# Cross-attention with MLP: scores from two float32r parts in half of the array's rows, each score matmul beside a row-maximum matmul

## The chip, the core and the metric

One core of a Trainium2 chip runs the kernel in one launch. Its engines run their own instruction streams and meet at semaphores: TensorE (PE in the profile, with its weight loads as PEld), VectorE (DVE), ScalarE (ACT), GpSimd (POOL), and SyncE (SP), which here issues all the DMAs. The metric is the device time of a run in microseconds, less is better, as the median of several runs.

## The reference

```python
qn = _layer_norm(Q, ln_q_g, ln_q_b)
q = (qn @ Wq + bq).reshape(B, Lq, H, DH).transpose(0, 2, 1, 3)
k = (KV @ Wk + bk).reshape(B, Lkv, H, DH).transpose(0, 2, 1, 3)
v = (KV @ Wv + bv).reshape(B, Lkv, H, DH).transpose(0, 2, 1, 3)
scores = jnp.einsum('bhqd,bhkd->bhqk', q, k) / jnp.sqrt(jnp.float32(DH))
attn = jax.nn.softmax(scores, axis=-1)
ctx = jnp.einsum('bhqk,bhkd->bhqd', attn, v)
ctx = ctx.transpose(0, 2, 1, 3).reshape(B, Lq, D)
x = Q + (ctx @ Wo + bo)
h = _layer_norm(x, ln_ff_g, ln_ff_b)
ff = jax.nn.silu(h @ W1 + b1) @ W2 + b2
return x + ff
```

All arrays are float32: 16 batches, 512 queries, 1601 keys, width 256, 16 heads of 16 numbers, an MLP of width 1024.

## The kernel before

The main loop has 16 batches of four quarters. A quarter is four heads: for each of 13 tiles of 128 keys (the last has 65) it makes scores with keys on the partitions and 512 queries along the row, two heads at a time. Such a half tile is a **unit**, so a quarter has 26 units and a batch 104. ScalarE takes the exponential of a unit (L717, 128x1024); after the second unit of a tile, TensorE multiplies the previous tile's probabilities by V (L1029, "pv"): four heads side by side in four groups of 32 array columns, float32.

The exponential needs the maximum of each query's scores subtracted. So TensorE makes the scores a second time, with queries on the partitions (L995, `make_rows`, in chunks of 512 keys, 52 steps for a quarter, every thirteenth of them four short products with the 65 last keys), into the two buffers of `rows_ps`, and VectorE reduces each step to a maximum (L830, `read_rows`). These maxima belong to the next quarter, or the one behind it; four steps fall to each key tile. In unit 19 VectorE negates and splits the finished maxima, in unit 22 TensorE turns them (kind "turn", L944), ScalarE copies them out, and SP places them by DMA as extra rows of `q_stack` (`place_shift`, L424), where the next quarter's first scores wait for them (`shift_landed`).

A float32 product of scores is made in bfloat16: q and k are each split into three bfloat16 parts (ScalarE writes `whole` and the first part, GpSimd subtracts for the others, L513 to L516), and the six products of parts that matter are stacked along the contraction: 6 x 16 = 96 rows, plus three for the shift. SP gathers the parts head by head into `k_stack` and `q_stack` (`place`, L389) and then copies the repeated ones (`repeat`, L401).

Every other product (projections k, q, v, output, both MLP layers, and transposes) is a float32 **side product** through one PSUM tile `side`, with an evacuation by ScalarE or VectorE. Tables give each a range of units. `plan` writes out TensorE's order: per key tile the scores, side products and pv, and between them the four maximum steps, spread evenly by the table `COST`. TensorE runs this order strictly: `make_rows` waits until VectorE has read the step before the last, `make_scores` until the exponential before the last is done.

A prologue prepares the first batch and its first maxima; an epilogue finishes the last batch's output and MLP.

Of the kernel before, what the change touches and what calls it, by code (L numbers as in the profile page):

```python
# [27 lines left out]
F32 = mybir.dt.float32  # L28
BF16 = mybir.dt.bfloat16
# [28 lines left out]
PLACED = 2 * 4 * PARTS  # L58
REPEATED = 2 * (len(K_ROWS) - PARTS)
# [64 lines left out]
def products(kind, arg):  # L124
# [4 lines left out]
    first, second = {"turn": (QT, 1), "x": (QT, 1), "k": (1, KC), "q": (1, KC), "wo": (2, 4), "h": (KC, 2), "w1": (2, KC), "w2": (2, FM)}[kind]  # L129
# [39 lines left out]
COST = {"scores": 512, "pv": 2048, "v": 512, "ctx": 256, "x": 256, "h": 256, "turn": 128, "k": 2048, "q": 2048,  # L169
        "wo": 1024, "w1": 1024, "w2": 1024}  # L170


def plan(steps):


    units, slot = [], 0
    for t in range(KT):
        work = []
        for u in (2 * t, 2 * t + 1):
            work += [(u, "scores", j) for j in range(2)]  # L180
            work += [(u, "side", product) for product in products_at(steps, u)]
            work += [(u, "pv", None)] * (u % 2)
        costs = [COST[what[1] if kind == "side" else kind] for _, kind, what in work]
        done, placed, tile = 0, 0, {2 * t: [], 2 * t + 1: []}
        for (u, kind, what), cost in zip(work, costs):
            tile[u].append((kind, what))
            done += cost
# [43 lines left out]
def xattn_kernel(nc, x, ctx, wq, bq, wk, bk, wv, bv, wo, bo, w1, b1, w2, b2, gq, cq, gf, cf, out):  # L231
    with ExitStack() as stack:
# [27 lines left out]
        rest = sb("rest", [P, CHUNK])  # L260
        k_parts = sb("k_parts", [P, PARTS, LK], BF16)
        q_parts = sb("q_parts", [P, PARTS, LQ], BF16)
# [100 lines left out]
        def _(sp):  # L363
# [70 lines left out]
            def prologue():  # L434
# [19 lines left out]
                for c in (2, 3):  # L454

                    sp.wait_ge(side_ready, index(PREPARE[1], "ctx", (c - 2, KC - 1)) + 1)
                    load_ctx(0, c)
# [659 lines left out]
```

## Time and profile before

| | us |
|---|---|
| runs: median of 3 (lowest to highest) | 3768.38 (3765.79 to 3769.14) |
| the profiled execution's own time | 3763.43 |
| its span, first to last instruction | 3761.6 |
| prologue, loop, epilogue (about) | 145, 3538, 79 |
| PE, DVE, ACT busy | 3559.0, 2483.2, 2242.9 |

Busy time counts an engine's instructions; waits on semaphores are not in it. A matmul's recorded duration contains the latency through the array, so the rate is read from starts: two matmuls in a row that start 0.22 us apart cost 0.22 us each, whatever their own duration says. Each float32 matmul stands in the trace as two records.

### The profile page before, as it was taken

The numbers are of one execution on the slowest core, as the hardware profiler recorded it, in microseconds if no ns is written. First come the engines' busy times: TensorE is split into PE (matmuls) and PEld (weight loads), VectorE is DVE, ScalarE is ACT, GpSimd is POOL, SyncE is SP. The second block draws the span as 40 slices with busy tenths as digits, with TensorE's granted clock in tenths as the row PEclk, the third lists the DMA queues.
The fourth block names the chain that finished last, engine by engine and source line by source line (L and its number), as shares of the span: only waits on it lengthen the run. The fifth ranks groups of instructions, "written<-read, shape, count | busy, mean of one in ns | idle before, by whom it ended". The sixth has DMA issues, their size and how long they took to land.

```text
span 3761.6 us, 52959 instructions
## 1 busy us (share of the span) xinstructions
PE 3559.0 (95%) x19880; PEld 1605.0 (43%) x19880; DVE 2483.2 (66%) x4568; ACT 2242.9 (60%) x2979; POOL 901.5 (24%) x1323
## 2 busy tenths in 40 slices
PE   3899999999999999999999999999999999999996
PEld 2233444444434444444444434444444444444434
DVE  2777767666676766667666676766667676676751
ACT  1366666656666565666656666566656656666562
POOL 2122313212231222313122231212313112231101
PEclk8899999999999999999999999999999999999999
DMA  3222212222122321212222122322212232121200
GB/s 84 45 50 40 46 32 61 41 47 45 32 51 39 65 41 32 47 33 58 41 58 38 30 50 37 64 41 36 49 32 54 42 64 39 27 48 34 41 7 12
DMA packets 121409, 162.99 MB, mean 43 GB/s; under 512 B 36912, under 2 KB 102464, under 8 KB 118080
## 3 DMA queue, kind: packets, MB, share of 16 engines
q1 hardware_dynamic: 121152, 159.60, 21.7%
q8 instruction: 157, 2.57, 0.3%
q14 instruction: 100, 0.82, 0.1%
HBM read 46.43 MB, written 8.39 MB: 15 GB/s over the span
## 4 chain that ended last, share of the span: by engine, by line
PE 81%; DVE 11%; ACT 4%; issue 2%; SPq 1%; POOL 1%; DMA 0%; ACTq 0%; POOLq 0%; DVEq 0%
PE o_ps L1029 20%; PE rows_ps L995 19%; PE scores L1010 14%; DVE chunk_max L830 8%; PE side L972 6%; PE side L969 6%; PE side L958 5%; PE side L950 4%; PE side L962 3%; ACT probs L717 2%; PE side L954 2%; DVE stats L748 1%; DVE resid L775 1%; PE side L941 1%; ACT ctxT L633 1%
## 5 line engine op out<-in xcount | busy, mean ns | idle before, releaser
L830 DVE TENSOR_REDUCE chunk_max<-rows_ps 128x1 f32<-128x512 f32 (+1 forms) x3328 | 2124.4, 666 | 1132.9 <-PE rows_ps L995 1124.4
L717 ACT ACTIVATE probs<-scores 128x1024 f32<-128x1024 f32 (+1 forms) x1664 | 1676.0, 1023 | 1174.5 <-PE scores L1010 1167.1
L995 PE MATMUL rows_ps<-k_stack,q_stack 96*128 96x512 bf16 (+1 forms) x4096 | 1220.1, 339 | 94.1 <-DVE chunk_max L830 50.6
L1010 PE MATMUL scores<-q_stack,k_stack 99*128 99x512 bf16 (+1 forms) x3328 | 1033.6, 379 | 3.3 <-ACT probs L717 2.7
L1029 PE MATMUL o_ps<-probs,v_sb 128*32 128x512 f32 x6656 | 886.5, 605 | 0.4 <-ACT probs L717 0.4
L995 PEld LDWEIGHTS rows_ps<-k_stack,q_stack 96*128 96x128 bf16 x4096 | 334.3, 97 | 1164.2 <-DVE chunk_max L830 930.7
L1010 PEld LDWEIGHTS scores<-q_stack,k_stack 99*128 99x128 bf16 (+1 forms) x3328 | 325.0, 100 | 300.4 <-issue 38.2
L513 POOL TENSOR_TENSOR rest<-whole,k_parts 128x512 f32<-128x512 f32 (+1 forms) x128 | 120.6, 942 | 1002.4 <-ACT k_parts L663 997.2
L565 POOL TENSOR_TENSOR attT<-o_sb,denom 128x512 f32<-128x512 f32 x64 | 81.2, 1268 | 945.3 <-DVE denom L817 945.3
L969 PE MATMUL side<-hT,w_sb 128*128 128x256 f32 x1024 | 272.6, 380 | 11.8 <-ACT tanh_sb L675 9.9
L972 PE MATMUL side<-w_sb,ffT 128*128 128x256 f32 x1024 | 259.2, 381 | 5.6 <-DVE ffT L793 5.0
L1029 PEld LDWEIGHTS o_ps<-probs,v_sb 128*32 128x32 f32 x6656 | 131.0, 108 | 296.8 <-issue 222.2
L958 PE MATMUL side<-wv_sb,ctxT 128*128 128x128 f32 (+1 forms) x1664 | 242.3, 278 | 4.6 <-ACT v_sb L649 2.0
L958 PEld LDWEIGHTS side<-wv_sb,ctxT 128*128 128x128 f32 (+1 forms) x1664 | 226.0, 187 | 46.7 <-ACT v_sb L649 11.4
L950 PE MATMUL side<-ctxT,wk_sb 128*128 128x512 f32 (+1 forms) x512 | 222.7, 519 | 9.2 <-ACT k_parts L663 9.2
L969 PEld LDWEIGHTS side<-hT,w_sb 128*128 128x128 f32 x1024 | 192.9, 190 | 63.2 <-ACT tanh_sb L675 17.0
L972 PEld LDWEIGHTS side<-w_sb,ffT 128*128 128x128 f32 x1024 | 191.5, 189 | 56.5 <-issue 7.7
L673 ACT ACTIVATE ffT<-side,half_b 128x256 f32<-128x256 f32 x256 | 121.5, 475 | 111.5 <-PE side L969 108.8
L528 POOL TENSOR_TENSOR newton<-rstd 128x2 f32<-128x2 f32 (+1 forms) x144 | 28.1, 195 | 591.6 <-DVE half_var L763 584.0
L962 PE MATMUL side<-wo_pad,attT 128*128 128x256 f32 x512 | 139.7, 389 | 5.0 <-POOL attT L565 3.9
L675 ACT ACTIVATE tanh_sb<-side,half_b 128x256 f32<-128x256 f32 x256 | 121.7, 475 | 0.0
L514 POOL TENSOR_TENSOR k_parts<-whole,k_parts 128x512 bf16<-128x512 f32 (+1 forms) x128 | 121.1, 946 | 0.1
(68 smaller groups left out, 1971.3 us busy)
## 6 DMA issues: line engine op xcount, KB each, us to landing
k_stack<-k_parts SPq DMA_DIRECT2D x768, 50.0 KB, 2.2
k_stack<-k_stack SPq DMA_DIRECT2D x192, 200.1 KB, 5.6
ctx_nat<-in_ctx SPq DMA_DIRECT2D x48, 512.0 KB, 4.0
q_stack<-q_parts SPq DMA_DIRECT2D x768, 16.0 KB, 1.8
q_stack<-q_stack SPq DMA_DIRECT2D x192, 64.0 KB, 3.4
x_nat<-in_x SPq DMA_DIRECT2D x16, 512.0 KB, 6.1
resid<-in_x SPq DMA_DIRECT2D x32, 256.0 KB, 2.8
out<-resid SPq DMA_DIRECT2D x32, 256.0 KB, 2.5
```

The source lines that it names most:

```text
L673: nc.scalar.activation(ffT[:, m, :], side[:, cols], ACT.Identity, bias=half_b1[:, m:m + 1], scale=0.5)
L675: last = nc.scalar.activation(tanh_sb[:, cols], side[:, cols], ACT.Tanh, bias=half_b1[:, m:m + 1], scale=0.5)
L717: nc.scalar.activation(probs[0:rows, (q + t) % 2, 2 * LQ * pair:2 * LQ * (pair + 1)], scores[0:rows, 2 * LQ * pair:2 * LQ * (pair + 1)], A ...
L830: nc.vector.tensor_reduce(dst, src, AX.X, ALU.max).then_inc(rows_read, 1)
L950: ins = nc.tensor.matmul(side[:, 0:width(arg)], wk_sb[:, j, P * s:P * (s + 1)], ctxT[:, j, CHUNK * arg:CHUNK * arg + width(arg)], start=(j ...
L958: ins = nc.tensor.matmul(side[0:rows, P * t:P * (t + 1)], ctxT[:, j, P * i:P * i + rows], wv_sb[:, j, P * s:P * (s + 1)], start=(j == 0), ...
L962: ins = nc.tensor.matmul(side[:, D * i:D * (i + 1)], attT[:, j, q0:q0 + P], wo_pad[:, j, :], start=(j == 0), stop=(j == 3))
L969: ins = nc.tensor.matmul(side[:, QH * i:QH * (i + 1)], w1_sb[:, j, P * m:P * (m + 1)], hT[:, j, :], start=(j == 0), stop=(j == KC - 1))
L972: ins = nc.tensor.matmul(side[:, D * i:D * (i + 1)], ffT[:, j, P * i:P * (i + 1)], w2_sb[:, j, :], start=(j == 0), stop=(j == FM - 1))
L995: last = nc.tensor.matmul(rows_ps[:, m % 2, d0:d0 + w], q_stack[s][0:STACK, h, P * t:P * (t + 1)], k_stack[s][0:STACK, h, k0:k0 + w], star ...
L1010: ins = nc.tensor.matmul(scores[0:keys_in(t), LQ * j:LQ * (j + 1)], k_stack[s][:, h, P * t:P * t + keys_in(t)], q_stack[s][:, h, :], start ...
L1029: last = nc.tensor.matmul(o_ps[32 * j:32 * j + 32, :], v_sb[q // 2][0:rows, t, col:col + 32], probs[0:rows, (q + t) % 2, LQ * j:LQ * (j + 1)],
```

## The change

q and k are split into two float32r parts (4 bytes each) in place of three bfloat16 ones; three products of parts are stacked, 48 rows plus two for the shift. A head then needs only half of the array's 128 rows: even heads stand in partitions 0 to 49 of the stacks, odd heads in 64 to 113. The maximum steps alternate between the halves. In each unit TensorE issues scores of the odd head, a maximum step of an even head, scores of the even head, a maximum step of an odd head; then pv in every second unit; then all of the unit's side products. The copies of repeated parts (`repeat`) are gone, since `place` now places all three; `place_shift` issues four DMAs in place of three; GpSimd has one subtraction in place of three per chunk; VectorE's negation has three instructions in place of seven; a turn is one float32 transpose in place of four bfloat16 matmuls. The short maximum products have 66 keys in place of 65.

```diff
-PARTS = 3
-K_ROWS = (0, 0, 0, 1, 1, 2)
-Q_ROWS = (0, 1, 2, 0, 1, 0)
+PARTS = 2
+K_ROWS = (0, 0, 1)
+Q_ROWS = (0, 1, 0)
 STACK = 16 * len(K_ROWS)
 ROWS = STACK + PARTS
+HALF = 64
+PAIRS = HH // 2
...
-TAIL = width(NCH - 1)
-M_STEPS = [step for r in range(M_ROWS) for step in [(r, c) for c in range(NCH - 1)] + [(r, None)] * (r % 4 == 3)]
+TAIL = width(NCH - 1) + 1
+M_STEPS = [step for p in range(2) for step in
+           [(e, p, t, c) for t in range(QT) for c in range(NCH - 1) for e in range(2)] + [(e, p, None, None) for e in range(2)]]
...
+PARTNER = (1, 0, 1, 0)
...
-    units, slot = [], 0
+    units = []
     for t in range(KT):
-        work = []
-        for u in (2 * t, 2 * t + 1):
-            work += [(u, "scores", j) for j in range(2)]
-            work += [(u, "side", product) for product in products_at(steps, u)]
-            work += [(u, "pv", None)] * (u % 2)
...
-            while placed < PER_TILE and done * PER_TILE >= (placed + MAX_PHASE) * sum(costs):
-                tile[u].append(("max", slot))
-                placed, slot = placed + 1, slot + 1
-        units += [tile[2 * t], tile[2 * t + 1]]
+        for n, u in enumerate((2 * t, 2 * t + 1)):
+            unit = []
+            for k in (2 * n, 2 * n + 1):
+                unit += [("scores", PARTNER[k]), ("max", PER_TILE * t + k)]
+            units.append(unit + [("pv", None)] * n + [("side", product) for product in products_at(steps, u)])
     return units
...
-        k_parts = sb("k_parts", [P, PARTS, LK], BF16)
-        q_parts = sb("q_parts", [P, PARTS, LQ], BF16)
-        k_stack = [sb(f"k_stack{s}", [ROWS, HH, LK], BF16) for s in range(2)]
-        q_stack = [sb(f"q_stack{s}", [ROWS, HH, LQ], BF16) for s in range(2)]
+        k_parts = sb("k_parts", [P, PARTS, LK], F32R)
+        q_parts = sb("q_parts", [P, PARTS, LQ], F32R)
+        k_stack = [sb(f"k_stack{s}", [P, PAIRS, LK], F32R) for s in range(2)]
+        q_stack = [sb(f"q_stack{s}", [P, PAIRS, LQ], F32R) for s in range(2)]
...
-                for part in range(PARTS):
-                    slot = rows.index(part)
+                for slot, part in enumerate(rows):
                     for h in range(4 * (g % 2), 4 * (g % 2) + 4):
-                        sp.dma_start(dst[16 * slot:16 * slot + 16, h, :], src[16 * h:16 * h + 16, part, :])\
...
+                        first = HALF * (h % 2) + 16 * slot
+                        sp.dma_start(dst[first:first + 16, h // 2, :].bitcast(F32),
+                                     src[16 * h:16 * h + 16, part, :].bitcast(F32)).then_inc(placed[g], 16)
...
                 place(k_stack[s], k_parts, K_ROWS, 2 * s + 1)
-                repeat(b, 2 * s)
                 place(q_stack[s], q_parts, Q_ROWS, 2 * s + 1)
-                repeat(b, 2 * s + 1)
...
-                for i in range(PARTS):
-                    sp.dma_start(q_stack[q // 2][STACK + i:STACK + i + 1, 4 * g:4 * g + 4, :],
-                                 shift_parts[4 * i:4 * i + 4, :])\
-                        .then_inc(shift_landed, 16)
+                for e in range(2):
+                    for i in range(PARTS):
...
-                wait(pool, split, b * 10 + n)
-                seq.inc(nc.gpsimd.tensor_tensor(rest[:, 0:w], src, first, ALU.subtract))
-                seq.inc(nc.gpsimd.tensor_tensor(second, src, first, ALU.subtract))
-                pool.wait_ge(pool_seq, seq.value)
-                nc.gpsimd.tensor_tensor(parts[:, 2, off:off + w], rest[:, 0:w], second, ALU.subtract).then_inc(split, 1)
+                nc.gpsimd.tensor_tensor(parts[:, 1, off:off + w], whole[:, n % 2, 0:w],
+                                        parts[:, 0, off:off + w].bitcast(F32), ALU.subtract).then_inc(split, 1)
...
-                    ins = nc.tensor.matmul(side[0:4 * PARTS, P * i:P * (i + 1)],
-                                           neg_parts[:, i, :, :].rearrange("p a h -> p (a h)"), ident_bf[:, :],
-                                           start=True, stop=True)
+                    ins = nc.tensor.transpose(side[0:PARTS * M_ROWS, 0:P],
+                                              neg_parts[:, :, :].bitcast(F32).rearrange("p a r -> p (a r)"), ident[:, :])
...
-                for row in [r] if c is not None else range(r - 3, r + 1):
-                    t, h = row // 4, 4 * (q % 2) + row % 4
-                    k0, w, d0 = (CHUNK * c, CHUNK, 0) if c is not None else (CHUNK * (NCH - 1), TAIL, TAIL * (row - r + 3))
-                    last = nc.tensor.matmul(rows_ps[:, m % 2, d0:d0 + w], q_stack[s][0:STACK, h, P * t:P * (t + 1)],
-                                            k_stack[s][0:STACK, h, k0:k0 + w], start=True, stop=True)
+                for tile in [t] if c is not None else range(QT):
+                    k0, w, d0 = (CHUNK * c, CHUNK, 0) if c is not None else (LK - TAIL, TAIL, TAIL * tile)
+                    last = nc.tensor.matmul(rows_ps[:, m % 2, d0:d0 + w], q_stack[s][rows, pair, P * tile:P * (tile + 1)],
+                                            k_stack[s][rows, pair, k0:k0 + w], start=True, stop=True)
...
-                j = 2 * (u % 2) + n
-                h = 4 * (q % 2) + j
+                j, pair, rows = 2 * (u % 2) + n, 2 * (q % 2) + u % 2, slice(HALF * n, HALF * n + ROWS)
                 ins = nc.tensor.matmul(scores[0:keys_in(t), LQ * j:LQ * (j + 1)],
-                                       k_stack[s][:, h, P * t:P * t + keys_in(t)], q_stack[s][:, h, :],
+                                       k_stack[s][rows, pair, P * t:P * t + keys_in(t)], q_stack[s][rows, pair, :],
                                        start=True, stop=True)
```

The order on TensorE where a k projection (L950 before, L921 after) is made; L1010 and L978 are scores, L995 and L964 maximum steps, L1029 and L997 pv. Before:

```order
L995 MATMUL rows_ps<-k_stack,q_stack 128x512 [waits rows_read]
L1010 MATMUL scores<-q_stack,k_stack 128x512 [waits exp_done]
L1010 MATMUL scores<-q_stack,k_stack 128x512
L995 MATMUL rows_ps<-k_stack,q_stack 128x512 [waits rows_read]
L950 MATMUL side<-ctxT,wk_sb 128x512 [waits side_read]
L995 MATMUL rows_ps<-k_stack,q_stack 128x512 [waits rows_read]
L1010 MATMUL scores<-q_stack,k_stack 128x512 [waits exp_done]
L1010 MATMUL scores<-q_stack,k_stack 128x512
L950 MATMUL side<-ctxT,wk_sb 128x512
L995 MATMUL rows_ps<-k_stack,q_stack 128x512 [waits rows_read]
```

Changed, the same place:

```order
L978 MATMUL scores<-q_stack,k_stack 128x512 [waits exp_done]
L964 MATMUL rows_ps<-k_stack,q_stack 128x512 [waits rows_read]
L978 MATMUL scores<-q_stack,k_stack 128x512
L964 MATMUL rows_ps<-k_stack,q_stack 128x512 [waits rows_read]
L997 MATMUL o_ps<-probs,v_sb 32x512 [waits exp_done]
L997 MATMUL o_ps<-probs,v_sb 32x512 x3
L921 MATMUL side<-ctxT,wk_sb 128x512
L978 MATMUL scores<-q_stack,k_stack 128x512 [waits exp_done]
L964 MATMUL rows_ps<-k_stack,q_stack 128x512 [waits rows_read]
L978 MATMUL scores<-q_stack,k_stack 128x512
L964 MATMUL rows_ps<-k_stack,q_stack 128x512 [waits rows_read]
L921 MATMUL side<-ctxT,wk_sb 128x512 [waits side_read]
```

Scores and maximum steps now alternate in fours at the head of each unit, and the float32 side products stand in a block behind them, where before a maximum step stood between them.

The order on TensorE from the turn (L944 before, L916 after) to the first scores of the next quarter, which wait for `shift_landed`. Before:

```order
L944 MATMUL side<-ident_bf,neg_parts 12x128 [waits max_negated,side_read]
L944 MATMUL side<-ident_bf,neg_parts 12x128 x3
L1010 MATMUL scores<-q_stack,k_stack 128x512 [waits exp_done]
L995 MATMUL rows_ps<-k_stack,q_stack 128x512 [waits rows_read]
L1010 MATMUL scores<-q_stack,k_stack 128x512
L1029 MATMUL o_ps<-probs,v_sb 32x512 [waits exp_done]
L1029 MATMUL o_ps<-probs,v_sb 32x512 x3
...
L995 MATMUL rows_ps<-k_stack,q_stack 128x512 [waits rows_read] x2
L1010 MATMUL scores<-q_stack,k_stack 128x512 [waits exp_done,shift_landed]
```

Changed:

```order
L916 MATMUL side<-ident,neg_parts 32x128 [waits max_negated,side_read]
L978 MATMUL scores<-q_stack,k_stack 128x512 [waits exp_done]
L964 MATMUL rows_ps<-k_stack,q_stack 128x512 [waits rows_read]
L978 MATMUL scores<-q_stack,k_stack 128x512
L964 MATMUL rows_ps<-k_stack,q_stack 128x512 [waits rows_read]
L997 MATMUL o_ps<-probs,v_sb 32x512 [waits exp_done]
...
L997 MATMUL o_ps<-probs,v_sb 32x512 [waits exp_done]
L997 MATMUL o_ps<-probs,v_sb 32x512 x3
L978 MATMUL scores<-q_stack,k_stack 128x512 [waits exp_done,shift_landed]
```

The turn stood between a unit's scores and the maximum step before; now it stands behind both pairs. The three units between it and the wait are the same units.

SP's queue while one set of stacks is filled. Before:

```order
L389 DMA k_stack<-k_parts 16x1601 x12
L389 DMA q_stack<-q_parts 16x512 x12
L389 DMA k_stack<-k_parts 16x1601 x12
L401 DMA k_stack<-k_stack 16x6404 x3
L401 DMA q_stack<-q_stack 16x2048 x3
L389 DMA q_stack<-q_parts 16x512 x12
L401 DMA k_stack<-k_stack 16x6404 x3
L401 DMA q_stack<-q_stack 16x2048 x3
L424 DMA q_stack<-shift_parts 1x4x512 x3
```

Changed:

```order
L381 DMA k_stack<-k_parts 16x1601 x12
L381 DMA q_stack<-q_parts 16x512 x12
L381 DMA k_stack<-k_parts 16x1601 x12
L381 DMA q_stack<-q_parts 16x512 x12
L404 DMA q_stack<-shift_parts 1x8x128 x4
```

The twelve copies within the stacks are gone, and the shift has one DMA more.

## Rows read from the trace of the kernel before

**Rows 1.** The page: busy us, share, instructions; TensorE's granted clock in tenths.
```profile
span 3761.6 us, 52959 instructions
PE 3559.0 (95%) x19880; PEld 1605.0 (43%) x19880; DVE 2483.2 (66%) x4568; ACT 2242.9 (60%) x2979; POOL 901.5 (24%) x1323
...
PEclk8899999999999999999999999999999999999999
```

**Rows 2.** Windows: prologue, loop behind its first batch, epilogue; busy us by engine.
```profile
0.00:145.00 145.00, 73.44 (x213) 30.55 (x213) 65.15 (x88) 20.74 (x38) 41.31 (x57) 0.78 0.29 63
...
367.00:3683.00 3316.00, 3230.11 (x18268) 1458.40 (x18266) 2247.80 (x4169) 2068.96 (x2740) 800.30 (x1181) 1.00 0.22 43
3683.00:3762.00 79.00, 43.97 (x176) 33.23 (x176) 13.00 (x29) 15.22 (x38) 16.31 (x33) 0.91 0.02 7
```

**Rows 3.** Windows: one batch in the loop, PE, PEld, DVE, ACT, POOL.
```profile
1252.00:1473.00 221.00, 215.57 (x1219) 97.61 (x1218) 150.53 (x280) 137.96 (x184) 55.20 (x82) 1.00 0.23 44
```

**Rows 4.** Timeline of PE, one key tile: start, us, line, operation.
```profile
1868.30 0.38 PE L995 MATMUL rows_ps<-k_stack,q_stack 96*128 96x512 bf16 x1
1868.61 1.06 PE L1029 MATMUL o_ps<-probs,v_sb 128*32 128x512 f32 x8
1869.61 0.39 PE L995 MATMUL rows_ps<-k_stack,q_stack 96*128 96x512 bf16 x1
1869.83 0.60 PE L1010 MATMUL scores<-q_stack,k_stack 99*128 99x512 bf16 x2
1870.27 0.38 PE L995 MATMUL rows_ps<-k_stack,q_stack 96*128 96x512 bf16 x1
1870.49 1.02 PE L950 MATMUL side<-ctxT,wk_sb 128*128 128x512 f32 x2
1871.35 0.38 PE L995 MATMUL rows_ps<-k_stack,q_stack 96*128 96x512 bf16 x1
```

**Rows 5.** Timeline of PE: a short maximum step of four matmuls and what follows.
```profile
1861.15 0.30 PE L995 MATMUL rows_ps<-k_stack,q_stack 96*128 96x65 bf16 x4
1861.28 1.10 PE L950 MATMUL side<-ctxT,wk_sb 128*128 128x512 f32 x2
```

**Rows 6.** The chain that ended last: eight float32 records of 128 columns.
```profile
1576.70 0.97 PE side L958 x8
```

**Rows 7.** Timelines of DVE and ACT: instructions of one kind back to back.
```profile
1857.03 2.52 DVE L830 TENSOR_REDUCE chunk_max<-rows_ps 128x1 f32<-128x512 f32 x4 [0.50 <-PE rows_ps L995]
...
1858.43 1.93 ACT L717 ACTIVATE probs<-scores 65x1024 f32<-65x1024 f32 x2 [1.62 <-PE scores L1010]
```

**Rows 8.** A turn: PE, ACT and SP timelines, and the next quarter's first scores.
```profile
1854.53 0.39 PE L944 MATMUL side<-ident_bf,neg_parts 128*12 128x128 bf16 x4
...
1855.34 0.56 ACT L635 CAST shift_parts<-side 12x512 bf16<-12x512 f32 x1
...
1855.92 1.91 SPq L424 DMA_DIRECT2D q_stack<-shift_parts  x3
...
1860.42 0.59 PE L1010 MATMUL scores<-q_stack,k_stack 99*128 99x512 bf16 x2
```

**Rows 9.** The page's DMA issues: KB each, us from issue to landing.
```profile
k_stack<-k_parts SPq DMA_DIRECT2D x768, 50.0 KB, 2.2
...
q_stack<-q_parts SPq DMA_DIRECT2D x768, 16.0 KB, 1.8
```

**Rows 10.** Prologue: SP's placements, the chain's POOL splits, TensorE's first maximum step.
```profile
67.92 7.84 SPq L389 DMA_DIRECT2D q_stack<-q_parts  x12
...
65.54 1.13 POOL q_parts L514
66.74 1.17 POOL q_parts L516
...
91.92 1.01 PE L995 MATMUL rows_ps<-k_stack,q_stack 96*128 96x512 bf16 x2 [18.72 <-DMA q_stack<-q_stack]
```

More of the change, by code:

```diff
@@ L28 @@
 F32 = mybir.dt.float32
-BF16 = mybir.dt.bfloat16
+F32R = mybir.dt.float32r
 I32 = mybir.dt.int32
@@ L128, in products @@
         return [(t, kc) for t in tiles_in(c) for kc in (range(KC) if kind == "v" else [arg[1]])]
-    first, second = {"turn": (QT, 1), "x": (QT, 1), "k": (1, KC), "q": (1, KC), "wo": (2, 4), "h": (KC, 2), "w1": (2, KC), "w2": (2, FM)}[kind]
+    first, second = {"turn": (1, 1), "x": (QT, 1), "k": (1, KC), "q": (1, KC), "wo": (2, 4), "h": (KC, 2), "w1": (2, KC), "w2": (2, FM)}[kind]
     return [(i, j) for i in range(first) for j in range(second)]
@@ L310, in xattn_kernel @@
         placed = [sem(f"placed{g}") for g in range(4)]
-        stack_landed = [sem(f"stack_landed{g}") for g in range(4)]
         scores_ready = sem("scores_ready")
@@ L507, in read_parts @@
                 parts, off = (k_parts, CHUNK * use) if use < NCH else (q_parts, 0)
-                src, first, second = whole[:, n % 2, 0:w], parts[:, 0, off:off + w], parts[:, 1, off:off + w]
                 pool.wait_ge(side_read, step_value(start, k))
-                wait(pool, split, b * 10 + n)
-                seq.inc(nc.gpsimd.tensor_tensor(rest[:, 0:w], src, first, ALU.subtract))
-                seq.inc(nc.gpsimd.tensor_tensor(second, src, first, ALU.subtract))
-                pool.wait_ge(pool_seq, seq.value)
-                nc.gpsimd.tensor_tensor(parts[:, 2, off:off + w], rest[:, 0:w], second, ALU.subtract).then_inc(split, 1)
+                nc.gpsimd.tensor_tensor(parts[:, 1, off:off + w], whole[:, n % 2, 0:w],
+                                        parts[:, 0, off:off + w].bitcast(F32), ALU.subtract).then_inc(split, 1)
             def follow(ins):
@@ L634, in side_step @@
                 elif kind == "turn":
-                    last = nc.scalar.copy(shift_parts[:, :], side[0:4 * PARTS, :])
+                    last = nc.scalar.copy(shift_parts[:, :], side[0:PARTS * M_ROWS, 0:P])
                 elif kind == "x":
@@ L835, in negate_maxima @@
                 dve.wait_ge(rows_read, per_quarter(len(M_STEPS), b, q, len(M_STEPS)))
[L836 to L844 removed]
+                link(nc.vector.tensor_reduce(neg_max[:, :], chunk_max[:, :, :], AX.X, ALU.max, negate=True))
+                link(nc.vector.tensor_copy(neg_parts[:, 0, :], neg_max[:, :]))
+                nc.vector.tensor_tensor(neg_parts[:, 1, :], neg_max[:, :], neg_parts[:, 0, :].bitcast(F32),
+                                        ALU.subtract).then_inc(max_negated, 1)
             def prologue():
@@ L1010, in make_scores @@
                 ins = nc.tensor.matmul(scores[0:keys_in(t), LQ * j:LQ * (j + 1)],
-                                       k_stack[s][:, h, P * t:P * t + keys_in(t)], q_stack[s][:, h, :],
+                                       k_stack[s][rows, pair, P * t:P * t + keys_in(t)], q_stack[s][rows, pair, :],
                                        start=True, stop=True)
-                if n == 1:
+                if not first:
                     ins.then_inc(scores_ready, 1)
```

70 lines of the change are left out of this document (23 added, 47 removed).

## The prediction

> **What bounds the kernel now.** I read the page first: PE is busy 95% of the span, DVE 66%, ACT 60%, and the granted clock is at full speed (2.4 GHz) but for the first slice [rows 1]. Then the windows: the loop is about 3538 of 3762 us, and in it a batch takes 221 us, in which PE is busy 215.5, DVE 150.5 and ACT 138.0 [rows 2, 3]. So TensorE's queue sets the loop's time; only 5.5 us of a batch are lost to waits and unevenness. The recorded durations overlap, so I take rates from starts in the timeline. From there, for one record each [rows 4 to 6]:
> - bf16, 512 columns (a score or a maximum step): 1870.27 to 1870.49, 0.217 us.
> - float32, 512 columns: 0.86 for two records, 0.43 each, four times the bf16 time per matmul.
> - pv: 1.00 us from its first record to what follows, and 0.31 in place of 0.22 from the matmul ahead of it. The same eight records one after the other in the whole array would take 8 x 0.43 = 3.4 us: four groups of columns do run at once, and going in costs 0.09 us and coming out 1.00 - 0.86 = 0.14.
> - four short bf16 products, 65 columns with a weight load each: 0.13 us, 0.033 each.
> - float32, 128 columns with a weight load of 128 columns: 0.97 / 8 = 0.121 us.
>
> DVE's maxima come 0.61 us apart when they are back to back (2.52 - 0.69 over three), ACT's exponentials 0.93 apart [rows 7].
>
> **The change, part by part, per batch.** Scores are 4 x 52 = 208 matmuls, maximum steps 192 long and 16 short. Before: 400 x 0.217 + 16 x 0.13 = 88.9 us.
>
> *The pair.* No row shows a float32r matmul or two halves of rows at once. Bounds for one pair (a score and a maximum step): from below 0.217 us, one bf16 record with the other hidden; from above 2 x 0.86 = 1.73, two float32 matmuls in turn. I take float32r to stream like bf16: float32 costs four times bf16, as two parts by two parts would, and here the split is made by hand and each matmul carries only products of single parts. I take the halves to run at once, since pv's four column groups do [rows 4]. But the weights now have 4 bytes, and the nearest row for such a load gives 0.121 us against 0.033 for bf16 [rows 5, 6]; two loads per pair in one port make 0.24, a little over the 0.217 of streaming. So: pair 0.24. A short step has four loads in one half, 4 x 0.121 = 0.48, where 0.13 stood, and its score 0.12. Sum: 192 x 0.24 + 16 x 0.60 = 55.7 us. **Gain 33.2 us.**
>
> The Trainium skill (TensorE: Matmul & The Clock Gate, Weight-path perf modes) says the fast weight load works for no float32 input, and gives P / 1.2, 107 ns, for 128 columns; by it a pair would be 0.21 to 0.22 and a short step 0.43. This trace agrees within its 0.121.
>
> *Switches between array layouts.* Side products need the whole array, pv four column groups, the pairs two row groups. Before, there was one way in and out of pv per tile. Of the 52 even units 40 now have a block of side products behind their pairs (two switches more), of the 52 odd ones 30 (one more): 110 switches. Pv's row prices one at 0.09 to 0.14 [rows 4]; for a change of row groups no row exists. I take 0.10: **loss 11 us**; bounds 0 (no drain between these layouts) and 22.
>
> The Trainium skill speaks against this part of the change (TensorEngine Tiling (Array Packing), Key Properties): changing the tiling mode, not just the tile, drains TensorE. Pv's 0.09 fits it. Without that rule the sum would be 11 us a batch lower.
>
> *Turn.* Four matmuls in 0.32 us [rows 8] become one of about 0.15: gain 0.7 a batch. TensorE's own work: 215.5 - 33.2 + 11 - 0.7 = **192.6 us**.
>
> *Unevenness.* Maxima stand now in twos at the head of each unit. I added up each of the 104 units: PE by the prices above, DVE 0.61 per step plus its other work, ACT 0.93 plus evacuations of 0.5 to 1.6. Before, the longer of DVE and ACT passes PE in 29 units, together by 9.3 us; the loop lost 5.5, or 0.59 of it, the rest being smoothed by the double buffers. Now it does so in 31 units, together by 15.1: in eleven even units without side products PE needs 2 x 0.24 = 0.48 and two maxima 1.22 (8.1 us), in the four units of the turn 0.83 against 1.24 (1.6), and ACT or VectorE passes it by less in sixteen others (5.4). With the same 0.59: **8.9 us**, so 201.5. In full it would be 15.1.
>
> *The shift.* Before: turn at 1854.53, SP's three issues end at 1857.83, landing about 1.8 us later at 1859.6, scores at 1860.42 [rows 8, 9]; the slack is 0.8. Now the three units between have no float32 work in two of four quarters and take 6 x 0.61 = 3.7 us by DVE's pace, where there were 5.9. The way is: ACT free behind the unit's exponential, 0.6; copy 0.3; four issues of 1.91 / 3 = 0.64, 2.5; landing 1.8: 5.2 us. So some 1.5 us are waited for in two quarters, part of it DVE's backlog: **2.5 us**. A batch: 204.0, or 17.0 less than 221.
>
> *At no cost.* GpSimd's two dropped subtractions, VectorE's four dropped instructions and SP's dropped copies lie beside TensorE's work in the loop; the bytes per stack stay about the same (three placements of 100 KB where one of 50 and a copy stood), and a quarter's maxima need them only in unit 20. If a place landed late there, TensorE would stop with everything behind it; the fill of 48 issues at about 0.65 takes 31 us from a quarter's start, of which the first 24 matter, 16 us against some 38 to unit 20.
>
> *Prologue.* The first maximum step waits 18.7 us for the copies and starts at 91.9 [rows 10]. Two of three splits go (2.3 us here, more for the k chunks before it), and so does the wait for the second set of k and the copies: the q placements start at 67.9 and last 7.8, and with 1.8 of landing the first step could go at about 75 less 3. From there VectorE's pace rules. **Gain 20 us.** The epilogue is float32 alone and stays.
>
> **Sum.** 16 x 17.0 + 20 = 292. The profiled execution took 3763.4 us, so 3471; the median of the runs is 5 us above it: **3475 us**.
>
> **Rivals.**
> 1. *The halves don't run at once* (slower). TensorE runs its matmuls in order, and every row of before uses all rows of the array; pv shows it for columns only. The pair is then 0.434, the matmuls of the first part cost 94.5 in place of 88.9 (5.6 more), and the switches remain: 215.5 + 5.6 + 11 - 0.7 = 231.4, with unevenness (5.5 x 0.59) and shift 235.6. 16 x 14.6 - 20 = +214: **3980 us**. It decides from a pair of 0.35 us on, where the loop's gain is used up.
> 2. *float32r streams at half rate*, as a float32 record does (0.43 per 512 columns), with the halves at once: the same pair, **3980**; at the whole float32 price (0.86) the pair costs 120 us a batch more than in the sum: about 5400. For it: the bytes are the same. Against it: four times bf16 is explained by the products of parts alone. The skill (FP8 and Floating Point Precision, TensorE Precision Notes) has true float32 as four passes and a reduced form that is read as 4 bytes and truncated; by it the stream is one pass, as I took it.
> 3. *Partly at once*, pair 0.30 to 0.35: each maximum step waits for VectorE while its partner score is half through. **3600 to 3760.**
> 4. *Unevenness in full*, the block of pairs leaving VectorE idle behind every long side block: 6.2 us a batch more, **3575**. With weight loads wholly hidden (0.217) it would be **3415**. Both are within the forecast's own range, as are switches at nothing (3300) or double (3650).
>
> **How the numbers follow.** Forecast with 4 and both switch bounds: 0.70, own range 3300 to 3650. Case 3: 0.10. Rival 1: 0.10, rival 2: 0.09. No change beyond 0.2%, about what a measurement here can tell: 0.01. The range of 3300 to 3760 leaves out rivals 1 and 2 and little below. Faster 0.79, same 0.01, slower 0.20.
>
> **What would show it.** Pairs of L978 and L964 whose starts lie a few ns apart, and pairs 0.24 apart; 0.12 per load in the short steps; 0.1 us more at each edge of a side block; PE waiting for DVE at L964 in units without side products; first scores of half of the quarters waiting for the shift; first maximum step near 72 us; a batch of 204 us. Starts of L978 and L964 always 0.2 us apart or more would prove rival 1, long lone records rival 2.

## The result

The changed kernel takes 4201.0 us (median of four runs, 4178.7 to 4237.3), the kernel before 3767.1: a ratio of 1.116, 95% interval 1.108 to 1.125. It is 434 us slower, where I had forecast 292 us less. The profiled execution took 4213.9 us.

The page of the changed kernel, busy time by engine and the granted clock, to be set against [rows 1]:

```profile
span 4211.9 us, 51519 instructions
PE 3857.4 (92%) x19688; PEld 1805.5 (43%) x19688; DVE 2423.7 (58%) x4312; ACT 2249.2 (53%) x2979; POOL 617.4 (15%) x1002
...
PEclk7798998989999789997889989899997998989888
```

The work of DVE and ACT is nearly what it was. What is new is the clock row: it dips all through the loop. The mean granted clock is 0.902 where it was 0.989, and it has two levels, so half speed (1.2 GHz) was granted for 2 x (1 - 0.902) x 4212 = 825 us, against 83 before. Two stretches of windows show one batch, against [rows 3], and one of the dips (PE, PEld, DVE, ACT, POOL, clock):

```profile
1520.70:1778.40 257.70, 240.68 (x1234) 111.39 (x1230) 150.35 (x269) 140.08 (x186) 38.42 (x62) 0.90 0.18 39
...
500.00:534.00 34.00, 30.02 (x162) 15.57 (x160) 18.23 (x32) 17.92 (x28) 0.00 (x0) 1.00 0.07 18
534.00:544.00 10.00, 9.96 (x31) 2.90 (x31) 5.11 (x8) 3.75 (x4) 0.00 (x0) 0.51 0.10 28
```

A batch takes 257.7 us, not 204, with 17.0 us in which TensorE is idle, where there were 5.5. TensorE's timeline around that dip (start, duration, what ended the idle time):

```profile
529.89 1.13 PE L940 MATMUL side<-hT,w_sb 128*128 128x256 f32 x4
530.95 0.49 PE L978 MATMUL scores<-q_stack,k_stack 50*128 50x512 f32 x1
530.95 0.73 PE L964 MATMUL rows_ps<-k_stack,q_stack 48*128 48x512 f32 x2
531.30 0.40 PE L978 MATMUL scores<-q_stack,k_stack 50*128 50x512 f32 x1
532.68 0.28 PE L916 MATMUL side<-ident,neg_parts 128*32 128x128 f32 x1 [0.99 <-ACT tanh_sb L651]
...
534.01 0.71 PE L964 MATMUL rows_ps<-k_stack,q_stack 48*128 48x512 f32 x1 [0.39 <-DVE chunk_max L807]
534.65 1.94 PE L997 MATMUL o_ps<-probs,v_sb 128*32 128x512 f32 x8
536.51 0.69 PE L978 MATMUL scores<-q_stack,k_stack 50*65 50x512 f32 x1
```

Four things are to be seen. The side block of four records of 256 columns takes 1.06 us to the next start, where four times 0.217 is 0.87: its first record in the new layout and the way out of it cost 0.19 together. The halves do run at once: a score and a maximum step both start at 530.95, the next pair 0.35 later. TensorE then stands for 0.99 us, because the next side product needs the PSUM tile that ScalarE is still evacuating, and for 0.39 on VectorE. And at 534 the clock is at half: pv takes from 534.65 to 536.51, 1.86 us, where it takes 1.00 at full clock.

The waits of the page's queues, longest first in total (us, times, longest):

```profile
PEld rows_ps L964 <- DVE chunk_max L807: 438.3, 653, 2.0
...
PE rows_ps L964 <- DVE chunk_max L807: 169.0, 287, 1.5
...
PEld side L921 <- ACT k_parts L639: 105.2, 93, 6.3
...
PE side L921 <- ACT k_parts L639: 66.8, 93, 5.5
```

93 waits of the k projection (L921) for `k_parts` have appeared; before, L950 waited 9.2 us for it in three waits.

### The profile page after: what moved, and what is told of

Same layout as the page of the kernel before. It is cut to its first block, busy times and chain, and to the rows that moved or that the text cites. A ratio compares the mean times of both kernels' runs of the same rounds, so it can differ in the third digit from the quotient of the medians.

```text
span 4211.9 us, 51519 instructions
## 1 busy us (share of the span) xinstructions
PE 3857.4 (92%) x19688; PEld 1805.5 (43%) x19688; DVE 2423.7 (58%) x4312; ACT 2249.2 (53%) x2979; POOL 617.4 (15%) x1002
## 4 chain that ended last, share of the span: by engine, by line
PE 80%; DVE 8%; ACT 7%; issue 3%; SPq 1%; POOL 0%; DMA 0%; ACTq 0%; POOLq 0%; DVEq 0%
PE o_ps L997 20%; PE scores L978 16%; PE rows_ps L964 12%; PE side L940 7%; PE side L943 6%; PE side L921 6%; PE side L929 6%; DVE chunk_max L807 5%; PE side L933 3%; ACT tanh_sb L651 2%; PE side L913 2%; ACT ffT L649 2%; DVE ffT L769 2%; PE side L925 2%; ACT k_parts L639 1%
## 5 line engine op out<-in xcount | busy, mean ns | idle before, releaser
L964 PE MATMUL rows_ps<-k_stack,q_stack 48*128 48x512 f32 (+1 forms) x4096 | 1467.8, 449 | 172.9 <-DVE chunk_max L807 169.0
L978 PE MATMUL scores<-q_stack,k_stack 50*128 50x512 f32 (+1 forms) x3328 | 1330.3, 475 | 3.7 <-ACT probs L693 2.2
L997 PE MATMUL o_ps<-probs,v_sb 128*32 128x512 f32 x6656 | 997.4, 674 | 0.4 <-ACT probs L693 0.4
L978 PEld LDWEIGHTS scores<-q_stack,k_stack 50*128 50x128 f32 (+1 forms) x3328 | 562.6, 197 | 760.7 <-issue 450.0
L964 PEld LDWEIGHTS rows_ps<-k_stack,q_stack 48*128 48x128 f32 x4096 | 645.9, 202 | 456.2 <-DVE chunk_max L807 438.3
L493 POOL TENSOR_TENSOR k_parts<-whole,k_parts 128x512 fp32r<-128x512 f32 (+1 forms) x128 | 132.6, 1036 | 1411.9 <-ACT k_parts L639 1410.4
L921 PE MATMUL side<-ctxT,wk_sb 128*128 128x512 f32 (+1 forms) x512 | 252.1, 588 | 66.8 <-ACT k_parts L639 66.8
L997 PEld LDWEIGHTS o_ps<-probs,v_sb 128*32 128x32 f32 x6656 | 136.0, 112 | 260.4 <-issue 234.5
L921 PEld LDWEIGHTS side<-ctxT,wk_sb 128*128 128x128 f32 x512 | 79.2, 199 | 201.9 <-ACT k_parts L639 105.2
L638 ACT ACTIVATE whole<-side,bk_c 128x512 f32<-128x512 f32 (+1 forms) x128 | 76.5, 598 | 161.6 <-PE side L921 155.5
L769 DVE SCALAR_TENSOR_TENSOR ffT<-tanh_sb,ffT 128x512 f32<-128x512 f32 x128 | 92.5, 722 | 105.7 <-ACT tanh_sb L651 105.7
L625 ACT COPY v_sb<-side 128x512 f32<-128x512 f32 (+1 forms) x128 | 64.8, 506 | 152.2 <-PE side L929 152.2
```

Of the source, the lines that this page charges most:

```text
L493: nc.gpsimd.tensor_tensor(parts[:, 1, off:off + w], whole[:, n % 2, 0:w], parts[:, 0, off:off + w].bitcast(F32), ALU.subtract).then_inc(sp ...
L769: nc.vector.scalar_tensor_tensor(z, tanh_sb[:, :], 1.0, z, ALU.add, ALU.mult).then_inc(silu_done, 1)
L921: ins = nc.tensor.matmul(side[:, 0:width(arg)], wk_sb[:, j, P * s:P * (s + 1)], ctxT[:, j, CHUNK * arg:CHUNK * arg + width(arg)], start=(j ...
L964: last = nc.tensor.matmul(rows_ps[:, m % 2, d0:d0 + w], q_stack[s][rows, pair, P * tile:P * (tile + 1)], k_stack[s][rows, pair, k0:k0 + w] ...
L978: ins = nc.tensor.matmul(scores[0:keys_in(t), LQ * j:LQ * (j + 1)], k_stack[s][rows, pair, P * t:P * t + keys_in(t)], q_stack[s][rows, pai ...
L997: last = nc.tensor.matmul(o_ps[32 * j:32 * j + 32, :], v_sb[q // 2][0:rows, t, col:col + 32], probs[0:rows, (q + t) % 2, LQ * j:LQ * (j + 1)],
```

## The experiments

The kernels ran in groups on a chip each, beside the kernel before, whose median there lay between 3766 and 3769 us every time; differences from it are taken within the group. "The changed kernel" is the one of the diff; only what differs from it is shown, unless the text says otherwise. A median comes from four runs, except 1 (one), 8 (six) and 9 (ten).

**1. Everything in one half.** The odd heads' scores and maxima are computed from the even heads' numbers.

```diff
-                s, pair, rows = q // 2, 2 * (q % 2) + p, slice(HALF * e, HALF * e + STACK)
+                s, pair, rows = q // 2, 2 * (q % 2) + p, slice(0, STACK)
```
and likewise in `make_scores`.

> Every score and maximum step reads rows 0 to 49 (0 to 47) of the stacks, so the odd heads' numbers are wrong; the work, the waits and the order are those of the changed kernel. In the changed kernel a pair starts within 4 ns and pairs follow 0.334 us apart. If the halves really run at once, they can't here: two matmuls 0.22 us apart or more (0.33 if a 4-byte weight load of 0.11 is exposed for each), a unit's block 0.88 to 1.3 us in place of 0.66, 104 blocks a batch, so 4201 + 16 x 104 x 0.22 = 4570 or more, less what fewer waits and a steadier clock give back. If the overlap in the changed kernel were only an artefact of how ends and starts are recorded, the time stays at 4200.

Measured: 4823.3 us in one run, clock 0.866. TensorE's timeline, one unit behind a side block and ahead of pv:

```profile
2001.35 0.50 PE L978 MATMUL scores<-q_stack,k_stack 50*128 50x512 f32 x1
2001.69 0.39 PE L964 MATMUL rows_ps<-k_stack,q_stack 48*128 48x512 f32 x1
2001.92 0.39 PE L978 MATMUL scores<-q_stack,k_stack 50*128 50x512 f32 x1
2002.15 0.39 PE L964 MATMUL rows_ps<-k_stack,q_stack 48*128 48x512 f32 x1
2002.47 1.06 PE L997 MATMUL o_ps<-probs,v_sb 128*32 128x512 f32 x8
```

So a lone float32r matmul of 512 columns streams in 0.23 us, as fast as bfloat16: rival 2 of the prediction is out. The block takes 1.12 us in place of 0.66, and the kernel 622 us more, at a clock below the changed kernel's 0.90: the overlap is real, rival 1 is out too. And the rows show something else: only the first matmul behind the side block takes 0.34.

**2. Two bfloat16 parts in the same halves.** `F32R = mybir.dt.bfloat16`, with the bitcasts gone and the turn as one bfloat16 matmul. The scores are coarser.

> The changed kernel with its two parts kept in bfloat16 (2 bytes) in place of float32r; scores are coarser for it, the rows, the halves, the order and the number of matmuls are the same. Weights theory: the 0.112 us by which a pair (0.334) exceeds one stream (0.217) is a 4-byte weight load that nothing hides; with 2-byte weights a pair is 0.22 to 0.25, a unit's block 0.45 to 0.5, some 16 us a batch of TensorE's work less. If TensorE then waits for VectorE instead, the time moves less than 250 us: 3950 to 4150. Rival, a fixed price of two halves at once or of leaving a layout: the pair stays at 0.33 and the time at 4200.

Measured: 3869.1 us, 332 less than the changed kernel, clocks of 0.952 to 0.961. Its block ahead of a side product:

```profile
2001.62 0.39 PE L982 MATMUL scores<-q_stack,k_stack 50*128 50x512 bf16 x1
2001.62 0.60 PE L968 MATMUL rows_ps<-k_stack,q_stack 48*128 48x512 bf16 x2
2001.85 0.38 PE L982 MATMUL scores<-q_stack,k_stack 50*128 50x512 bf16 x1
2002.16 1.99 PE L937 MATMUL side<-wo_pad,attT 128*128 128x256 f32 x8
```

0.23 to the second pair and 0.31 from it to the side product: 0.54 for the block. The weights theory holds in that the 0.11 us goes with 2-byte weights. The gain is larger than the 250 us that I expected at most. 104 blocks a batch that are 0.12 shorter are 200 us; the rest stands beside the clock, which rose from 0.90 to 0.96. TensorE waits longer for VectorE than in the changed kernel, 231.9 us where it was 169.0.

**3. pv behind the side products.**

```diff
-            units.append(unit + [("pv", None)] * n + [("side", product) for product in products_at(steps, u)])
+            units.append(unit + [("side", product) for product in products_at(steps, u)] + [("pv", None)] * n)
```

> pv of an odd unit stands behind its side products in place of ahead of them. Wait theory: in the changed kernel TensorE stands still at the first product of a side step, because ScalarE still evacuates the step before, with only a 0.66 us block of pairs in between; with pv (1.0 us) in between too, the waits of L921 for k_parts (66.8 us) and of L940 (25 us) go, and with fewer gaps the granted clock rises from 0.90. Expected 4201 less 90 to 250 us: 3950 to 4110. Rival: the loss is work (pairs of 0.33, layout switches) and VectorE's waits, then the time stays within 30 us of 4200.

Measured: 3899.1 us, 302 less; clocks of 0.948 to 0.970. The wait theory holds, beyond its range. The wait for the evacuation is gone from the same view, the one for VectorE is not:

```profile
PE rows_ps L964 <- DVE chunk_max L807: 151.3, 320, 1.2
...
PE side L921 <- ACT k_parts L639: 7.4, 3, 4.6
```

Its timeline shows two units without side products in a row, four pairs:

```profile
2004.47 0.50 PE L978 MATMUL scores<-q_stack,k_stack 50*128 50x512 f32 x1
2004.48 0.73 PE L964 MATMUL rows_ps<-k_stack,q_stack 48*128 48x512 f32 x2
2004.81 0.62 PE L978 MATMUL scores<-q_stack,k_stack 50*128 50x512 f32 x2
2005.76 0.49 PE L964 MATMUL rows_ps<-k_stack,q_stack 48*128 48x512 f32 x1 [0.33 <-DVE chunk_max L807]
```

The second group of two scores begins at 2004.81 and ends at 2005.43; a score's record is 0.39 long, so its second one began at 2005.04. The first pair took 0.34, the second 0.23. The extra 0.11 is paid once, at the entry into the halves, and not per pair. The gain is not one of layouts. An odd unit passes from the halves to pv, the whole array and the halves again in one order, and from the halves to the whole array, pv and the halves in the other: three changes each. In the traces of both kernels a block of pv takes 1.00 us and a side block of four records of 256 columns 1.06, whatever stands in front.

**4. More work in the bare units.** The step's matmul is issued twice in even units without side products, with the same result.

```diff
-                for tile in [t] if c is not None else range(QT):
+                for tile in [t] * (1 + twice) if c is not None else range(QT):
```

> In the fifteen even units of a batch that have no side products (or the turn alone) each maximum step's matmul is issued twice, with the same result: only more work for TensorE where it waits for VectorE, 15 x 2 x 0.22 = 6.6 us a batch, 106 us in all. Clock theory: gaps in these units make the granted clock fall to 1.2 GHz (830 us of the span in the changed kernel, 83 before); filling them keeps it up, so the time falls in spite of more work, to 3950 to 4150, with a mean clock of 0.94 or more. Rival: the clock's fall costs little, or comes from elsewhere; then the time is 4200 to 4310 and the clock stays at 0.90.

Measured: 4209.7 us, 9 more, at clocks of 0.916 to 0.926. Inconclusive between the two as put: the clock rose, but less than the theory had it, and the work was paid back without gain. And the edit did not do what it was for. VectorE can read a step only when its second matmul is done, so the wait can move with it; the view of waits has as much as in the changed kernel (169.0 us, 287 times):

```profile
PE rows_ps L964 <- DVE chunk_max L807: 175.5, 331, 1.6
```

So this run does not show what the clock does when these waits are gone.

**5. The kernel before in the grouped order.** Three bfloat16 parts, 96 rows, and `plan` as in the changed kernel (scores 0, step, scores 1, step, pv, side products).

> The kernel before, three bfloat16 parts in 96 rows, with the order of the changed kernel alone: score, maximum step, score, maximum step at the head of each unit, then pv, then the side products. Order theory (the grouping itself makes waits: for evacuations at side steps, for VectorE in bare units): the time rises to 3850 to 3950 although no matmul got dearer, and the granted clock falls under 0.98. Rival (grouping is harmless, the loss comes from float32r and the halves): 3767 within 30 us.

Measured: 3997.1 us, 229 more than the kernel before (ratio 1.061, 1.059 to 1.063), at clocks of 0.986 to 0.988. The order alone costs more than half of the loss, 47 us beyond the expected range, and without the fall of the clock that was expected with it. Busy time and TensorE's waits:

```profile
PE 3665.0 (92%) x19880; PEld 1600.0 (40%) x19880; DVE 2464.1 (62%) x4568; ACT 2266.6 (57%) x2979; POOL 906.9 (23%) x1323
...
PE rows_ps L986 <- DVE chunk_max L821: 129.7, 250, 1.3
...
PE side L941 <- ACT k_parts L654: 55.3, 93, 7.7
```

The same 93 waits for `k_parts` are here. And its timeline prices the way into a float32 block, once from a block in the same layout, once from pv:

```profile
2003.66 1.03 PE L960 MATMUL side<-hT,w_sb 128*128 128x256 f32 x4
2004.53 0.38 PE L1001 MATMUL scores<-q_stack,k_stack 99*128 99x512 bf16 x1
...
2005.50 1.06 PE L1020 MATMUL o_ps<-probs,v_sb 128*32 128x512 f32 x8
2006.49 1.13 PE L960 MATMUL side<-hT,w_sb 128*128 128x256 f32 x4
2007.46 0.38 PE L1001 MATMUL scores<-q_stack,k_stack 99*128 99x512 bf16 x1
```

0.87 us without a change of layout, 0.97 behind pv; the 0.99 of pv itself is what it is everywhere. So the first float32 record behind a change of layout costs 0.10 more than one without a change.

**6. The changed kernel in the spread order.** `COST` and `plan` of the kernel before, with the scores of the odd head first.

> The changed kernel (two float32r parts, halves) with the spread order of the kernel before: maximum steps between side products, evenly by the table of costs; scores of the odd head first. Order theory: fewer waits, a clock near 0.98; but a maximum step that stands alone has no partner and costs 0.22 plus a layout switch of 0.09 to 0.11 at each side. If waits and clock weigh more than the lost overlap: 3900 to 4100. If the lost overlap weighs more: 4200 to 4500.

Measured: 4244.7 us, 44 more than the changed kernel, at clocks of 0.938 to 0.947. Spreading doesn't help the halves, although the clock is higher: a step that stands alone has no partner and pays the entry. In this run's timeline one starts at 2001.39, and the pv behind it at 2001.81, 0.42 us later.

**7. Halves that change with every matmul.**

```diff
-            for k in (2 * n, 2 * n + 1):
-                unit += [("scores", PARTNER[k]), ("max", PER_TILE * t + k)]
+            unit = [("scores", 0), ("scores", 1)] + [("max", PER_TILE * t + k) for k in (2 * n, 2 * n + 1)]
```

> The changed kernel with a unit's four matmuls in the order scores even head, scores odd head, maximum step even, maximum step odd, so that the half changes with every matmul; in the changed kernel the halves go odd, even, even, odd. Staircase theory: the 4-byte weights of a matmul are loaded (0.11 us) only when the one ahead of it has started, so a second half starts 0.11 behind the first; with halves odd, even, even, odd the third waits for the second's end (0.33), while with strictly changing halves each starts 0.11 behind the last and a block is 3 x 0.11 + 0.22 = 0.55 in place of 0.66. 104 blocks, 16 batches: 4201 less about 180 us where no wait takes it back, 4000 to 4100. Rival, two weight loads for each pair are a price of the port whatever the order: the block stays at 0.66 and the time within 30 us of 4200.

Measured: 4260.8 us, 60 more. The staircase theory fell:

```profile
2003.51 0.50 PE L976 MATMUL scores<-q_stack,k_stack 50*128 50x512 f32 x2
2003.85 0.40 PE L962 MATMUL rows_ps<-k_stack,q_stack 48*128 48x512 f32 x2
...
2004.94 0.66 PE L919 MATMUL side<-ctxT,wk_sb 128*128 128x65 f32 x4 [0.69 <-ACT k_parts L637]
```

Pairs still go in twos, 0.34 apart for the first. Where nothing waits, the block stays at 0.67 us. What changes is that the maxima come to VectorE one pair later; TensorE's waits for it grow from 169.0 to 237.5 us.

**8. Both together, float32r.**

> The order of e7 and pv behind the side products as in the third experiment (3899). If the two gains are apart (evacuations on one hand, weight loads on the other), 3899 less 100 to 180: 3720 to 3800, about the time of the kernel before (3768) or a little under it, with a clock of 0.95. If TensorE then waits for VectorE for what it saves (rows_ps has two buffers), 3850 to 3900.

Measured: 4088.1 us, 189 more than experiment 3. It lies above both ranges: the gain hoped for rested on the staircase, and TensorE waits 215.2 us for VectorE, where it was 151.3 in experiment 3.

**9. Both together, bfloat16 parts.**

> As the run before, with the two parts in bfloat16, so scores are coarser. It bounds what weights of 4 bytes still cost when the order is mended. Blocks of 0.45 to 0.54. The first bfloat16 run took 3869, pv behind gave 302 us to the changed kernel; if that gain is the evacuation's alone it comes here too: 3550 to 3650. If VectorE's pace is the bound by then (two buffers, maxima in twos), 3650 to 3800.

Measured: 3767.4 us (ratio 1.000, 0.999 to 1.001), in the range for VectorE's pace. TensorE waits 328.3 us for VectorE here, the most of all versions.

**10. The kernel before, grouped, with pv behind the side products.**

> The kernel before with the grouped order, as in the fifth experiment (3997), but pv behind the side products. If the place of pv (a side step's first product waits for the evacuation of the step before) is what the grouping costs, this returns to 3767 within 40 us. If pairs in twos starve VectorE as well, 3810 to 3900 remains.

Measured: 3822.0 us, 175 less than experiment 5 and 55 more than the kernel before. The place of pv is three quarters of what the order costs. The 55 us that remain lie in the range for pairs in twos; TensorE waits 87.5 us for VectorE here and 50.6 in the kernel before.

**11. Two bfloat16 parts, the changed kernel's order, pv behind.**

> Two bfloat16 parts (coarser scores) in halves, in the changed kernel's order of odd, even, even, odd, with pv behind the side products. The two changes gave 332 us (weights) and 302 us (pv) alone; if they are apart, 3567. The same kernel with both scores ahead of both maxima took 3767; if the 189 us that this order cost with float32r is VectorE getting its first maximum a pair later, the two orders differ by about as much here: 3560 to 3620. If it is bound by VectorE's pace anyway: 3700 or more.

Measured: 3652.1 us, ratio 0.969 (0.968 to 0.971), between the two ranges. It is the only version faster than the kernel before, with coarser scores; no version with float32r parts was. It is 115 us faster than experiment 9, whose only difference is the order of scores and steps; the gains of 2 and 3 overlap by 85 us.

**12. Experiment 3 with the doubled steps of experiment 4.**

> The changed kernel with pv behind the side products (3899, clock 0.948) and each maximum step's matmul twice in the fifteen bare units of a batch, some 110 to 130 us of added work. Clock theory: the slow stretches begin in these units, so the clock rises to 0.97 or more and the time stays at 3850 to 3920, the added work being paid back. Rival, the clock doesn't depend on these units: 3980 to 4030.

Measured: 3982.3 us, 83 more, at clocks of 0.955 to 0.959, inside the spread of experiment 3 (0.948 to 0.970). The time is the rival's. Its reading is not shown, for the waits for VectorE again stayed (150.7 us, 151.3 in experiment 3): the doubled steps didn't fill them.

## Why the prediction was wrong

Three terms of the sum failed: unevenness, which left out TensorE's longer waits behind a new order; the clock, which was put at nothing without a reason; and the switches, taken at half of what they cost.

**The clock** was the step that I did not have. The prediction noted full speed in [rows 1] and carried it over as given. Its price can be read from the changed kernel's own four runs: the slowest, 4237.3 us at 0.895, had 890 us at half speed, the fastest, 4178.7 at 0.912, had 735. That is 58.6 us of time for 155 us of slow clock, 0.38 each. By it the 807 us that the four runs have on average, against 83 before, cost about 275 us: at the clock of before the kernel would take about 3925. That is an extrapolation over four runs; no experiment held the clock at full speed in this kernel.

What brings the clock down is only narrowed. The profiled execution of the changed kernel has 68 falls to half speed in its loop. Ahead of 66 of them, TensorE's last wait of 0.3 us or more was one of L964 for VectorE, 0.71 us in the median; ahead of none was it one of L921 for `k_parts`. In experiment 3 the same holds for all 19. But most such waits are followed by no fall: the changed kernel has 255 of them at full clock, and experiment 5 has 169 and only four falls, 14 us in all. Nor is it the sum of waits. Experiment 3 waits less for VectorE and `k_parts` than experiment 5 (159 us, 185 us) and has 0.948 to 0.970 where that has 0.987.

Among the kernels with pairs in halves fewer waits go with a higher clock (0.902 to about 0.96 in experiment 3, 0.956 to 0.973 from 2 to 11). But experiment 1 waits least for VectorE of the kernels with halves (53.5 us), spends the longest in half of the rows, one matmul at a time, and has the lowest clock, 0.866; ahead of 23 of the 63 falls in its loop no wait of 0.3 us stands within 5 us, where in the changed kernel one stands ahead of all 68. So the runs point to the matmuls in halves first, and to waits for VectorE as what adds to them; no experiment took these waits away from the pairs.

**Unevenness** was mis-sized. I carried over 0.59 of the sum of what DVE and ACT exceed PE by, unit by unit, and got 3.4 us a batch more than before. That counts engines' work in a unit and no chain. The chain it missed: a side step's first product waits until ScalarE has evacuated the step before. In the order before, pv and a maximum step stood between the two; pv now stands ahead of the last product, with only a block of 0.66 us behind it. The changed kernel's trace shows it for a k projection, whose evacuation is two instructions, 1.3 us:

```profile
546.11 1.13 PE L921 MATMUL side<-ctxT,wk_sb 128*128 128x512 f32 x2
547.27 0.69 ACT L638 ACTIVATE whole<-side,bk_c 128x512 f32<-128x512 f32 x1 [1.03 <-PE side L921]
547.86 0.68 ACT L639 ACTIVATE k_parts<-side,bk_c 128x512 fp32r<-128x512 f32 x1
548.59 1.13 PE L921 MATMUL side<-ctxT,wk_sb 128*128 128x512 f32 x2 [0.70 <-ACT k_parts L639]
```

Experiment 5 prices the order at 229 us, 14.3 a batch, and experiment 10 puts 175 of it on the place of pv. Part of the 175 is the dearer first record of a side block behind pv (0.97 against 0.87 us in experiment 5), gone in 30 units: 30 x 0.1 x 16 = 48 us. The order rows ahead of the prediction show it: L997, then L921, and pairs on both sides.

**The pair** was right where I had thought it most doubtful: 0.23 us in the middle of a block against 0.24 forecast, halves at once, float32r at the rate of bfloat16. **The switches** were mis-sized: I took 0.10 for each of 110 and named double of that as the bound, and the bound is about what they cost where the next layout has 4-byte weights: 0.09 for the change (halves to pv 0.32 - 0.23) and 0.10 to 0.11 for the first weights, which nothing hides. A side block inside halves shows the sum, 0.19 for its own first record and the way out, plus 0.11 in the first pair behind it. With 0.1 more for each of the 110, and 0.1 for each of the 22 entries from pv that I had at nothing, that is 13 us a batch, 211 in all. Against it stand 6 us a batch, 98 in all, by which the pairs (0.23 for 0.24) and the short steps (0.34 with their score, for 0.60) came out cheaper than the sum had them. Experiment 2 took the entry away for the halves; its 332 us hold that, the cheaper short steps and the clock.

**Rival 3** (pairs of 0.30 to 0.35, 3600 to 3760) had the size of a block's first pair and another cause; the time lay far above. Rivals 1 and 2, which would have given 3980, are refuted by experiment 1.

**The shift** cost less than the 40 us forecast: scores wait 18.9 us in all for `shift_parts`, 17.5 of it ahead of a weight load, where they waited 2.2 before. **The prologue**: the first maximum step starts at 71.4 us, forecast near 72 (before: 91.9, [rows 10]), but the loop's first scores come at 136.3 in place of 145.5, a gain of 9 us and not 20. Between the two VectorE's pace and the work left to prepare rule. **The epilogue** stayed, 82 us against 79. No run shows a gain from GpSimd's, SP's and VectorE's savings, which the forecast put at nothing; none tests it.

The sum, then: 3475 forecast; 275 for the clock; 87 for the order (229 of experiment 5, less 94 that the forecast had for unevenness and shift, less 48 that it had for 30 switches from pv into side blocks, which experiment 5 has too); 163 for the other switches (211 less 48 for the same 30); 11 for the prologue; less 98 for pairs and short steps. That gives 3913. Some 290 of the 4201 us are in none of these terms.

The traces say where they are. I cut the loop into blocks, each a run of scores and steps, of pv, or of side products, from its first start to the next block's. A block of pairs without a wait is priced by the rows above, pv and side blocks by the fastest of their kind. What the blocks at full clock take beyond it I call waits, what the others take beyond the mean at full clock I call half clock. These are estimates from the starts in the profiled executions, in us, rounded:

| | loop | blocks | waits | half clock |
|---|---|---|---|---|
| the kernel before | 3540 | 3290 | 240 | 0 |
| experiment 5 | 3770 | 3350 | 410 | 10 |
| the changed kernel | 3990 | 3090 | 630 | 270 |
| experiment 3 | 3710 | 3090 | 480 | 140 |
| experiment 2 | 3660 | 2890 | 650 | 120 |

The forecast had the blocks 366 us cheaper than before, the waits 94 longer, and nothing for the clock. They came out 200 cheaper and 390 longer, and 270 for the clock, near what the four runs price it at. So waits and clock are the two large misses. Experiment 5 has 170 us of their growth, from the order alone; the rest came with the cheaper pairs, and that fits VectorE's pace: a block of 0.66 us holds two steps, and VectorE reads maxima 0.61 us apart [rows 7]. The line between blocks and waits depends on these prices, to some tens of us.

## What to carry to other kernels

Sum the chains across a reordered queue, not only each engine's work per slot: find for each product what frees its buffer, and what stands in between before and after. Work that is made cheaper than the pace of the engine that reads it comes back as waits. A side trip between two layouts pays at both ends, here 0.09 us for each change and 0.1 more for each entry with 4-byte weights; count the changes before and after. Where matmuls go into half of the array's rows, or TensorE will wait more often, put a price on the granted clock falling, from rows at both levels, before summing at full speed.

## What the runs showed that I had not expected

- Clock: with 93 waits for `k_parts` each and waits of 130 to 232 us for VectorE, 96-row bfloat16 matmuls kept 0.987 (experiment 5), pairs in halves 0.956 (bfloat16) and about 0.90 (float32r). Four runs of the changed kernel spread by 1.4% in step with their clocks, where the kernel before spreads by 0.1%.
- The first matmul in a new layout with 4-byte weights takes 0.34 us to the next, later ones 0.23; with 2-byte weights it is 0.23 from the first.
- The Trainium skill (TensorE: Matmul & The Clock Gate, HAM oscillation) warns that long idle gaps between matmuls bring the clock down. The dip shown above follows gaps of 0.99 and 0.39 us, and experiment 5, with gaps up to 1.3 us at its maximum steps, has only four short ones in its loop, while experiment 1, which of the kernels with halves waits least for VectorE, has the lowest clock: the gaps alone don't decide it in these runs.
